# Second cross attention: when the keys and values are projected, and how the keys are stacked

## What is computed

```python
qh = split(LN(x) @ W_q.T + b_q); kh = split(ctx @ W_k.T + b_k); vh = split(ctx @ W_v.T + b_v)   # 16 heads of 8
scores = einsum('bhqd,bhkd->bhqk', qh, kh) / sqrt(8)
attn = einsum('bhqk,bhkd->bhqd', softmax(scores), vh)
x = x + concat(attn) @ W_o.T + b_o
```

## Time and profile before

| | us |
|---|---|
| median of 3 runs (1412.51 to 1415.54) | 1412.52 |
| profiled execution, its own time | 1414.38 |
| profiled execution, its span | 1412.6 |
| PE busy in the span | 1337.2 (95%) |
| DVE, ACT, POOL busy | 1051.9, 863.9, 735.0 |
| stage of the change, first and last L1085 | 872.9 to 1276.7 |
| mean granted TensorE clock | 0.979 of full speed |

### The profile page before, as it was taken

The page is one execution under the profiler, slowest core; times in us unless marked ns, Lnnn a source line. Parts: engine busy times, 40 slices in busy tenths (PEclk is TensorE's granted clock), DMA queues, the critical chain, the costliest instruction groups (busy, mean ns, idle before and its releaser), DMA issues.

```text
span 1412.6 us, 25408 instructions
## 1 busy us (share of the span) xinstructions
PE 1337.2 (95%) x9220; PEld 1037.2 (73%) x9220; DVE 1051.9 (74%) x2127; ACT 863.9 (61%) x1849; POOL 735.0 (52%) x416
## 2 busy tenths in 40 slices
PE   7889999999999999999998987899999999999998
PEld 4548888888888888888875854566666666665687
DVE  6558778888778777888854577777778778785787
ACT  4537667666666666676632554466666666665675
POOL 5136443334444444433151374187887887884463
PEclk9999999999999999999998899899999999998999
DMA  3132222211122222221150130644645536440131
GB/s 86 60 94 52 57 58 58 53 39 41 47 56 58 52 57 58 57 58 28 44 160 2 59 77 25 142 119 103 140 111 120 144 88 147 97 96 2 59 109 42
DMA packets 71803, 104.39 MB, mean 74 GB/s; under 512 B 14670, under 2 KB 54934, under 8 KB 71550
## 3 DMA queue, kind: packets, MB, share of 16 engines
q1 hardware_dynamic: 60062, 91.39, 25.9%
q10 hardware_dynamic: 11616, 11.38, 2.9%
HBM read 63.65 MB, written 2.11 MB: 47 GB/s over the span
## 4 chain that ended last, share of the span: by engine, by line
PE 81%; DVE 9%; DMA 3%; ACT 3%; SPq 2%; issue 1%; ACTq 0%; POOL 0%; DVEq 0%; POOLq 0%
PE PS L702 10%; PE PS L716 6%; PE PS L690 5%; PE PS L1105 5%; PE PS L1085 5%; PE PS L1119 5%; PE PS L691 5%; PE PS L692 5%; PE PS L718 5%; PE PS L717 5%; PE PS L1044 3%; SPq L1277 2%; PE PS L1792 2%; PE PS L745 2%; PE PS L1794 2%; PE PS L1793 2%
## 5 line engine op out<-in xcount | busy, mean ns | idle before, releaser
L1234 POOL TENSOR_TENSOR QO_area<-QO_area,prob_a 125x896 f32<-125x896 f32 x150 | 315.2, 2101 | 100.2 <-DVE QO_area L1433 80.3
L868 ACT ACTIVATE HL<-PS 125x512 fp32r<-125x512 f32 (+1 forms) x384 | 206.6, 539 | 178.1 <-PE PS L702 161.3
L960 DVE TENSOR_TENSOR HL<-PS,HL 125x512 fp32r<-125x512 f32 (+1 forms) x384 | 238.1, 622 | 74.5 <-ACT HL L868 53.4
L1410 DVE TENSOR_REDUCE QO_area<-PS 112x1 f32<-112x500 f32 x384 | 237.4, 670 | 44.3 <-PE PS L1085 44.1
L1329 ACT ACTIVATE prob_a<-PS 125x448 f32<-125x448 f32 x384 | 187.6, 540 | 122.6 <-PE PS L1105 117.3
L775 POOL TENSOR_TENSOR HL<-ctx_area,ones 125x512 fp32r<-125x512 f32 (+1 forms) x64 | 93.0, 1453 | 245.4 <-PE PS L718 191.5
L1085 PE MATMUL PS<-HL 96*112 96x500 f32 x384 | 157.8, 480 | 16.9 <-DVE QO_area L1410 12.1
L716 PE MATMUL PS<-HL 125*128 125x512 f32 (+1 forms) x384 | 155.7, 405 | 2.2 <-DVE HL L960 1.7
L690 PE MATMUL PS<-HL 128*128 128x500 f32 x336 | 152.8, 455 | 4.3 <-DVE HL L930 3.9
L878 ACT ACTIVATE prob_a<-prob_a,neg_max 128x500 f32<-128x500 f32 x192 | 135.5, 707 | 25.3 <-DVE neg_max L952 24.0
L718 PE MATMUL PS<-HL 125*128 125x512 f32 (+1 forms) x384 | 140.4, 366 | 0.0
(11 more groups left out here) (260 smaller groups left out, 2727.0 us busy)
## 6 DMA issues: line engine op xcount, KB each, us to landing
HL<-prob_b SPq DMA_DIRECT2D x128, 187.5 KB, 3.9
ctx_area<-in_ctx_T SPq DMA_DIRECT2D x16, 750.0 KB, 13.1
ctx_area<-in_ctx SPq DMA_DIRECT2D x16, 750.0 KB
HL<-ctx_area SPq DMA_DIRECT2D x64, 187.5 KB, 3.8
inv_area<-in_ctx_T SPq DMA_DIRECT2D x8, 750.0 KB, 4.1
prob_a<-in_ctx_T SPq DMA_DIRECT2D x8, 750.0 KB, 4.4
inv_area<-inv_kept ACTq DMA_DIRECT2D x16, 256.0 KB, 3.4
ctx_area<-in_L_ffn_W SPq DMA_DIRECT2D x16, 256.0 KB, 3.2
```

The source lines that it names most:

```text
L868: nc.scalar.activation(pH[k % 3][0:KC, 0:width(g)], PS[0:KC, 2 + k % 3, 0:width(g)], ACT.Copy)\
L960: nc.vector.tensor_tensor(pL[k % 3][0:KC, 0:width(g)], PS[0:KC, 2 + k % 3, 0:width(g)], pH[k % 3][0:KC, 0:width(g)].bitcast(fp32), ALU.sub ...
L1234: nc.gpsimd.tensor_tensor(acc, acc, late_p[n % LATE_P], ALU.add).then_inc(m["padd"], 1)
L1410: nc.vector.tensor_reduce(late_part[b % 2][:, u // NKB, u % NKB:u % NKB + 1], PS[0:2 * S, u % NKB, 0:KB], AX, ALU.max).then_inc(m["mx"], 1)
```

## The change

The six projections of a batch move to steps 2, 4, 6 (keys) and 8, 10, 11 (values). DVE takes the low part of a key piece one step after its projection, in steps 3, 5 and 7. The DMAs that stack the keys are issued for each piece of 500 keys alone, with a semaphore for each piece: 3 x 12 DMAs of 32 rows of 500 numbers. Who waited for `stack` waits for the piece that it uses: unit w of the maxima for piece w, ACT and DVE before they overwrite piece w.

```diff
+PROJECTED = (2, 4, 6, 8, 10, 11)
@@ maxima, PE
-                if u == 0:
-                    pe.wait_ge(m["stack"], 16 * 12 * (b + 1))
-                    if b:
-                        pe.wait_ge(m["qset"], b)
+                if u < NKB:
+                    pe.wait_ge(m[f"stack{w}"], 16 * 12 * (b + 1))
+                if u == 0 and b:
+                    pe.wait_ge(m["qset"], b)
@@ rest, PE
-                    if b + 2 < B and c in (2, 3, 4):
-                        project(b + 2, c - 2)
-                    if b + 2 < B and c in (6, 8, 10):
-                        project(b + 2, c // 2)
+                    if b + 2 < B and c in PROJECTED:
+                        project(b + 2, PROJECTED.index(c))
@@ stack, SP
-                sp.wait_ge(m["khi"], 3 * (b + 1))
-                sp.wait_ge(m["klo"], 3 * (b + 1))
-                if b >= 3:
-                    sp.wait_ge(m["sc"], 2 * NC * (b - 2))
-                for j in range(4):
-                    for r, half in enumerate((late_kH, late_kH, late_kL)):
-                        sp.dma_start(late_k[b % 3][r * QUAD:(r + 1) * QUAD, j * S2:(j + 1) * S2].bitcast(fp32),
-                                     half[j * QUAD:(j + 1) * QUAD, :].bitcast(fp32)).then_inc(m["stack"], 16)
+                for w in range(NKB):
+                    sp.wait_ge(m["khi"], 3 * b + w + 1)
+                    sp.wait_ge(m["klo"], 3 * b + w + 1)
+                    if b >= 3 and w == 0:
+                        sp.wait_ge(m["sc"], 2 * NC * (b - 2))
+                    for j in range(4):
+                        for r, half in enumerate((late_kH, late_kH, late_kL)):
+                            at = j * S2 + w * KB
+                            sp.dma_start(late_k[b % 3][r * QUAD:(r + 1) * QUAD, at:at + KB].bitcast(fp32),
+                                         half[j * QUAD:(j + 1) * QUAD, w * KB:(w + 1) * KB].bitcast(fp32))\
+                                .then_inc(m[f"stack{w}"], 16)
@@ keys, ACT and DVE
-                if b and piece == 0:
-                    act.wait_ge(m["stack"], 16 * 12 * b)
+                if b:
+                    act.wait_ge(m[f"stack{piece}"], 16 * 12 * b)
@@ rest, ACT
-                    if b + 2 < B and c in (2, 3, 4):
-                        keys(b + 2, c - 2, 7)
-                    if b + 2 < B and c in (6, 8, 10):
-                        values(b + 2, c // 2 - 3, 7)
+                    if b + 2 < B and c in PROJECTED[0:3]:
+                        keys(b + 2, PROJECTED.index(c), 7)
+                    if b + 2 < B and c in PROJECTED[3:6]:
+                        values(b + 2, PROJECTED.index(c) - 3, 7)
@@ rest, DVE
-                    if b + 2 < B and c in (2, 3, 4):
-                        keys(b + 2, c - 2, 7)
+                    if b + 2 < B and c - 1 in PROJECTED[0:3]:
+                        keys(b + 2, PROJECTED.index(c - 1), 7)
```

More of the change, by code:

```diff
@@ L285, in decoder_kernel @@
         ld_late = [sem(f"ld_late{i}") for i in range(2)]
-        names = ("wqrep qp qhi qlo q0set qset ones kmm khi klo stack vmm vev mxmm mx nmsplit nmtr nmcopy nmlow nmrow "
+        names = ("wqrep qp qhi qlo q0set qset ones kmm khi klo stack0 stack1 stack2 vmm vev mxmm mx nmsplit nmtr nmcopy nmlow nmrow "
                  "sc exp pv first padd sum norm wo out").split()
@@ L1400, in keys @@
                 dve.wait_ge(m["khi"], 3 * b + piece + 1)
-                if b and piece == 0:
-                    dve.wait_ge(m["stack"], 16 * 12 * b)
+                if b:
+                    dve.wait_ge(m[f"stack{piece}"], 16 * 12 * b)
                 c = slice(piece * KB, (piece + 1) * KB)
@@ L1880, in experts_sync @@
             sp.wait_ge(la["vmm"], 3 * B)
-            sp.wait_ge(la["stack"], 16 * 12 * B)
+            for w in range(NKB):
+                sp.wait_ge(la[f"stack{w}"], 16 * 12 * B)
             for e in range(E):
```

## The result

The changed kernel takes 1537.3 us (median of 4, 1532.5 to 1539.0), the kernel before 1412.9: a ratio of 1.087, 95% interval 1.084 to 1.090. It is slower by 124 us; the forecast was 1512 (+99). The profiled execution took 1539.0 us with a span of 1537.2.

A forecast was written before the change was run, and what follows sets the result against it. The prediction took the changed kernel to be bound by a chain through 36 stacking issues on SP's queue, 30.7 us a loop. +77 us for it and +22 for the low clock made +99: 1512 us, range 1430 to 1550.

The forecast's parts named there:

- A chain through SP's queue, closed by unit 2: Second cross attention: unit 2's release to the next takes 30.7 us through the stacking issues; PE waits about 6 us a loop.
- The price of an issue: Stacking DMAs on SP's queue: 0.635 us from start to start, the same with a third of the bytes.
- The train of 22.14 us: SP's 36 stacking issues for one batch: 22.14 us from SP's waking to the last start.
- The landing of 2.1 us: Time for a stacking copy to land: about 2.1 us, between 2.0 and 2.6.
- The clock, + 1.5 us a loop: PE's clock falls in each loop's wait, slowing steps 1 and 2: 1.5 us a loop, between 0 and 3.
- The first stacking: Batch 1's keys: the first release of unit 2 comes at 902.0, against 894.8 before, +7.2 us.
- the fifteenth clock term: The low clock was counted 15 times at 1.5 us, 22 us in the sum, beside 14 loops of the chain.
- The removed 0.87 and the returned 0.5 us: PE's step 3 low-part wait goes, 0.87 us a loop; 0.5 returns through VectorE's step 7; neither changes the time.
- Rival 1: Stacking issues take 0.40 to 0.46 us and stay hidden, so the kernel is faster: 1407 us; chance 0.14.
- rival 3: Issues near break-even at 0.48 us, gain and wait cancel: 1409 to 1416 us; chance 0.04.
- Rival 2: Slower, but with issues of 0.55 us or the clock staying full: 1446 to 1490 us; chance 0.14.
- Rival 4: The wait goes but VectorE becomes the bound; ruled out by 5 us, 19.9 us busy in a 25.3 us loop.

The follow-up runs named there:

- the pieces alone: Kernel before, with keys stacked in 36 DMAs and a semaphore for each piece, but projections and low parts in their old steps: 1523.8 us, ratio 1.075.
- the clock held: Changed kernel plus 7 unused matmuls of 448 columns in each loop, ahead of unit 2 of the maxima, where PE waits: 1508.3 us, ratio 1.064.
- the other order: Kernel before with its 12 DMAs, second key matmul behind step 3's products, third in step 5 between maxima and scores: 1424.2 us, ratio 1.006.
- two trains: Changed kernel with 24 instead of 36 stacking DMAs a batch, pieces 0 and 1 together, then piece 2: 1479.3 us, ratio 1.045.

## Why the prediction was right, and where its sizes were off

- *A chain through SP's queue, closed by unit 2.* Right: the wait stands where it was put, in step 1, at 6.1 to 7.8 us, 6.7 on average (forecast 6), in each loop; the experiment with the pieces alone has it too.
- *The price of an issue does not fall with the bytes.* Right: 0.633 us from start to start, forecast 0.635. The Trainium skill's rule to coalesce transfers under 64 KB ("DMA: Bandwidth & Descriptors", "Rules for kernel authors") agrees with this trace as to the pieces of 62.5 KB. The reason here is the time of SP's issues: each copy lands 2.0 us after its issue, and SP is at it for 23 us. 64 KB is no border here, since copies of 187.5 KB at the start of a train were issued at the same price. One step of the argument was weaker than it looked: the 0.33 us of the context's load, set against the copies, is the price with SP's queue empty before it. Directly behind the stacking train the same load takes 0.58:
```profile
872.91 0.34 SPq L1265 DMA_DIRECT2D inv_area<-in_ctx_T  x1
...
1002.68 0.58 SPq L1265 DMA_DIRECT2D inv_area<-in_ctx_T  x1
```

- *The train of 22.14 us.* Off by 1.1: first to last start is 22.6 to 24.9 us, 23.27 on average, because one or two issues in each of these trains take 1.1 to 1.8 us. That is 14 x 1.13 = 16 us.
- *The landing of 2.1 us.* Right: 2.05.
- *The clock, + 1.5 us a loop.* Mis-sized: low part 0 is ready 8.60 us after the release on average instead of 6.4 + 1.5. The clock stayed low over both of PE's steps that lie on the chain, in most loops; with the clock held it is 6.37. So this term had the right sign and cause, and the wrong size: it is 2.2 us, so 14 x 0.7 = 10 us are missing from the sum.
- *The first stacking.* Release at 904.9 instead of 902.0; the stage's first maxima matmul itself was at 875.8 instead of 872.9 in this execution.
- Train and clock together are + 1.8 us a loop (33.99 instead of 32.2): 25 us, which is what lies between 1512 and 1537. The smaller terms cancel: the late first release (+2.9), the fifteenth clock term of 1.5 in the sum, and 1.3 us less behind the last loop.
- *The removed 0.87 and the returned 0.5 us change nothing.* Right in the changed kernel. Where they count, with a semaphore for each group of heads, the new steps gain 10.2 us in the 14 loops, where 5 were forecast: 0.87 us goes and 0.21 of the forecast 0.5 comes back in step 9 (a wait of 0.69 us instead of 0.48). That the values which left step 6 let VectorE arrive earlier at step 7 may be why it is so little; this was not tested.
- *Rival 1*, issues that stay hidden, falls with the median of 591 ns, and *rival 3* with it. *Rival 2* needed issues of 0.55 us or a full clock; even with the clock held the time was 1508, above its 1490. *Rival 4*, VectorE, is out in the changed kernel; the other order shows how it comes in when an instruction that waits is put ahead of its reductions.

What stays open is how single issues come to take 1.1 to 1.8 us (20 of 576 in the changed kernel). The traces show what goes with them. Each of the 20 overlaps one packet of 16,384 bytes on the DMA queue q8, whose kind is "instruction" on the page; such a packet runs from 988.40 to 989.36, and the issue at 988.60 takes 1.12 us. In the stage 18 such packets fall on the stacking trains, each with one slow issue, and 6 fall between them. All 56 slow issues of the kernels with pieces only, with the clock held and with two trains overlap such a packet too. That the packet slows the issue is not shown by an experiment.

## What to carry to other kernels

Before a transfer is split so that its first part can be used sooner, multiply the number of issues by the price of one in a row of the trace, and put the train between the instruction that frees its source and the first that needs its last part: 36 x 0.63 us was hidden in no loop, though it is less than a loop. The slow issues belong to the price as well, here 1.1 us a train. To be ready sooner, wait for the transfers in the order in which they are used, with more semaphores and the same DMAs; that cost nothing here, took the queue off the path, and made the other half of the change worth 14 us. When an instruction is moved in the list of an engine that works in order, follow the wait in front of it: in the other order it moved to PE's next line. And where an engine stands still long enough for the clock to fall, price the steps behind the wait at the low clock if they are on the chain that ends it.

## What was not expected of the hardware

- A copy from SBUF to SBUF of 32 rows, behind another one, is issued in 0.59 us whether the rows have 4,000 or 2,000 bytes; with 6,000 that holds for the first few of a train, and later ones take about 0.9. A load of 128 rows from HBM with 750 KB takes 0.33 us with nothing just ahead of it in the queue, and 0.58 directly behind the train of small copies. So what stands ahead counts, and the bytes do not; what part the kind of source and destination has is not shown alone.
- After a wait of about 6.5 us PE's clock was at 1.2 GHz for 6.5 us more of full work (966.2 to 976.5, released at 969.98), and for 4.4 to 6.5 us in the others of the 14 loops. It fell as well around the waits of 2.9 to 4.1 us of the kernel with two trains. Around shorter ones it did so at times: in the kernel before with the wait of 1.7 us that ended at 921.1, not with one of 1.2 that ended at 999.6; with the clock held, with one of 2.4 us (1001.0) and not with another of 2.4 (1098.0). The length of the wait alone does not tell it.
- To fill the wait with matmuls that nobody reads took 29 us off a kernel.
